# Mixtures of experts: the standardized rows stored by SyncE on the hardware queue, ahead of the experts' weights

## What is computed

```
x = x + mamba(layernorm(x))
x = x + mixture0(layernorm(x))      # 32 experts, top 4
x = x + rotary_attention(layernorm(x))
x = x + mixture0(layernorm(x))
x = x + sink_attention(layernorm(x))
x = x + mixture1(layernorm(x))      # 48 experts kept, top 8, at most 96 rows each
x = x + latent_attention(layernorm(x))
x = x + mixture1(layernorm(x))
```

## Time and profile before

| | |
|---|---|
| median of 3 executions | 4134.72 us (4134.48 to 4136.27) |
| the profiled execution | 4140.78 us |
| its span, first to last instruction | 4138.2 us |
| PE busy | 3287.4 us, 79% of the span |
| DVE busy | 2811.4 us, 68% |
| ACT busy | 2274.7 us, 55% |
| POOL busy | 1809.1 us, 44% |
| mean granted PE clock | 0.871 |

### The profile page before, as it was taken

The page is one execution under the profiler, slowest core; times in us unless marked ns, Lnnn a source line. Parts: engine busy times, 40 slices in busy tenths (PEclk is TensorE's granted clock), DMA queues, the critical chain, the costliest instruction groups (busy, mean ns, idle before and its releaser), DMA issues. The chain is left out here.

```text
span 4138.2 us, 68603 instructions
## 1 busy us (share of the span) xinstructions
PE 3287.4 (79%) x19706; PEld 2595.8 (63%) x19707; DVE 2811.4 (68%) x6227; ACT 2274.7 (55%) x5958; POOL 1809.1 (44%) x3103
## 2 busy tenths in 40 slices
PE   7799958916888499089999999999737399999374
PEld 3355546715777377068778878788635288888253
DVE  5699956636777566468768778588553388888542
ACT  3599913405777244078768678688302266666021
POOL 0299923567663144636446356255237200000265
PEclk9799978958999599589999999999856699999566
DMA  2011132430000335300000000000234300000524
GB/s 84 20 48 49 49 144 89 136 101 13 1 1 1 144 114 131 113 29 19 17 11 20 14 14 19 11 17 20 112 86 67 102 1 1 1 1 1 180 51 105
DMA packets 133309, 221.35 MB, mean 53 GB/s; under 512 B 28912, under 2 KB 106608, under 8 KB 131264
## 3 DMA queue, kind: packets, MB, share of 16 engines
q1 hardware_dynamic: 99216, 147.84, 10.7%
q0 software_dynamic: 33792, 69.83, 7.4%
HBM read 162.60 MB, written 54.80 MB: 53 GB/s over the span
## 5 line engine op out<-in xcount | busy, mean ns | idle before, releaser
L1271 POOL DMA_INDIRECT ex_xr<-scratch_rows,mo_token x288 | 287.5, 998 | 324.8 <-issue 289.1
L596 POOL TENSOR_TENSOR sc_h<-sc_h,sc_c 128x512 f32<-128x512 f32 x256 | 327.2, 1292 | 198.1 <-DVE sc_h L633 190.2
L3044 DVE TENSOR_TENSOR sa_pT<-bank,sa_pT 128x512 fp32r<-128x512 f32 x512 | 329.9, 686 | 34.4 <-ACT sa_pT L2912 30.5
L2904 ACT ACTIVATE sa_p<-bank,sa_nm 128x512 f32<-128x512 f32 x512 | 346.9, 689 | 2.5 <-DVE sa_nm L3035 2.5
L633 DVE TENSOR_TENSOR_SCAN sc_h<-sc_da,bank 128x512 f32<-128x512 f32 x256 | 311.1, 1220 | 38.4 <-ACT sc_da L576 23.5
L2733 PE MATMUL bank<-sa_kT,sa_qT 128*128 128x512 f32 x1024 | 332.7, 436 | 1.5 <-DVE residual L3011 1.5
L3031 DVE TENSOR_REDUCE sa_mx<-bank 128x2 f32<-128x1024 f32 x256 | 312.4, 1220 | 25.6 <-PE bank L2735 21.7
L1337 PE MATMUL bank<-mo_w_gu,ex_xT 128*128 (+2 forms) x1152 | 315.0, 402 | 1.1 <-issue 0.6
L2757 PE MATMUL bank<-sa_pT,sa_v 128*128 128x256 f32 x2048 | 301.4, 290 | 17.1 <-DVE sa_pT L3044 16.4
L2757 PEld LDWEIGHTS bank<-sa_pT,sa_v 128*128 128x128 f32 x2048 | 260.2, 190 | 40.0 <-DVE sa_pT L3044 31.4
L2912 ACT ACTIVATE sa_pT<-bank 128x512 fp32r<-128x512 f32 x512 | 274.3, 585 | 7.7 <-PE bank L2745 0.5
(11 more groups left out here) (402 smaller groups left out, 9458.5 us busy)
## 6 DMA issues: line engine op xcount, KB each, us to landing
scratch_ys<-ex_yo SPq DMA_DIRECT2D x192, 128.0 KB
mo_w_gu<-in_w_gu SPq DMA_DIRECT2D x2, 9216.0 KB, 26.2
sc_c<-scratch_c SPq DMA_DIRECT2D x64, 256.0 KB, 3.1
sa_share<-scratch_shares SPq DMA_DIRECT2D x256, 64.0 KB, 2.6
mo_w_dn<-in_w_dn SPq DMA_DIRECT2D x2, 4608.0 KB, 47.5
mo_w_dn<-in_w_dn SPq DMA_DIRECT2D x2, 4096.0 KB, 34.7
scratch_rows<-ln_stage POOLq DMA_DIRECT2D x64, 128.0 KB, 21.9
ex_xr<-scratch_rows,mo_token POOLq DMA_INDIRECT x288
```

Of the source, the lines that this page charges most:

```text
L596: pool.tensor_tensor(h, h, C[u], ALU.mult).then_inc(used.sem, 1)
L1271: pool.indirect_dma_start(xr[u][:, :], None, rows, bass.IndirectOffsetOnAxis(ap=token[:, i:i + 1], axis=0), bounds_check=rows.shape[0] - 1 ...
L2904: act.activation(pr[h][:, :], SC[2 * s_ + h][:, :], ACT.Exp, bias=nm[:, col:col + 1], scale=SCALE, accum_out=rs[:, col:col + 1]).then_inc( ...
L3044: dve.tensor_tensor(spot(1), PT[h][:, :].rearrange("p (k n) -> p k n", k=TPB), spot(0).bitcast(F32), ALU.subtract).then_inc(*inc("kept_d"))
```

## The change

POOL no longer stores the standardized rows. SP does it, between `loads` and `late_loads`: for each tile it waits until DVE has made it and issues the store. Then come the experts' weights (and the copy of the residual). Last, SP waits within the block until all 16 stores have landed.

```diff
@@ -179,16 +179,16 @@
                         loads(sp)
                     if not c.fills:
                         zero_scratch(c, sp)
+                    if rows is not None:
+                        for i in range(TILES):
+                            sp.wait_ge(normed.sem, normed.at(i + 1))
+                            sp.dma_start(rows[0][i * P:(i + 1) * P, 0:D_MODEL], normal(i)) \
+                              .then_inc(rows[1][i % 4].sem, 16)
                     if late_loads is not None:
                         late_loads(sp)
-
-            if rows is not None:
-                @block.gpsimd
-                def _(pool):
-                    for i in range(TILES):
-                        pool.wait_ge(normed.sem, normed.at(i + 1))
-                        pool.dma_start(rows[0][i * P:(i + 1) * P, 0:D_MODEL], normal(i)) \
-                            .then_inc(rows[1][i % 4].sem, 16)
+                    if rows is not None:
+                        for u in range(4):
+                            sp.wait_ge(rows[1][u].sem, rows[1][u].at(16 * (TILES // 4)))
```

## The result

The changed kernel takes 4073.7 us (median of 4, 4072.2 to 4076.4) against 4135.5 us (median of 4, 4134.5 to 4141.4): a ratio of 0.985, 95% interval 0.983 to 0.987, or 62 us less. The forecast was 4075 us, with a range of 4066 to 4088.

What follows compares the result with a forecast made beforehand. Taken to bound the kernel: four waits, 62.3 us in all, at router openings, until POOL's row stores land. Less 4 x 0.6 us, the gain is 59.9, all other terms nil: 4134.7 - 59.9 = 4074.8 us, range 4066 to 4088.

Steps and rivals of the forecast that it cites:

- The cause of the holes: Router block's opening: all engines idle, 62.3 us in four waits, because POOL ends the layer-norm block only when its stores land.
- The first rival: Layer-norm block's end: rows land as late as before, since all queues share 16 DMA engines; no change, 4134.7 us; chance 0.03.
- The gain term: Four router openings: waits of 62.3 us shrink to 0.6 us each, a gain of 59.9 us.
- SP's issues: Layer-norm block: 16 added stores on SP per mixture at 0.4 us each, ending at 575.5 and 2991.9; no cost.
- The other stand-in: Layer-norm block: each row's store lands 3.5 us after its issue, as the tags do, the last at 579.0.
- The margins: Layer-norm block's end: rows land before DVE's last work by 12 us in the first mixture, 10 us in the third.
- The weights: Issued 16 to 17 us later, behind the stores; slack 36 us before PE, 16 us before POOL's first gather; no cost.
- The tags: Router block, second kind: behind the copy on SP's queue, landing by 3052.2 at the latest, slack 11 us; no cost.
- Load beside the router: Router's first 12 us (first kind) to 42 us (second) run under the weights' load; taken as 0, up to 7.8 us.

Runs made afterwards that it cites:

- `only_second_kind`: Against the kernel before: SP stores the rows in the two mixtures of the second kind alone, POOL still stores in the first kind; 4091.5 us, ratio 0.989.
- `pool_rows_made_first`: Against the kernel before: POOL still stores the rows, SP issues the weights once DVE has made the last tile; 4179.9 us, ratio 1.010.
- the last experiment: Against the changed kernel: SP issues weights and copy in the router block, only after DVE has counted the masks; 4103.6 us, ratio 0.992.
- `sp_weights_first`: Against the changed kernel: SP issues the weights and copy first and the row stores behind them, still waiting for the rows; 4144.6 us, ratio 1.0024.
- `copy_on_pool`: Against the changed kernel: in the second kind POOL issues the residual's copy after DVE's last tile, nobody in the block waiting for it; 4078.1 us, ratio 0.986.

## Why the prediction was right

**The cause of the holes.** The reading that POOL does not come to the end of a block before its own stores are done rested on two coincidences, given as 0.9 us; the landings unrounded make them 1.0. The trace before has them in all four mixtures: DVE goes on 0.98 to 0.99 us after POOL's last row is in. The two runs in which POOL stores beside the load (`only_second_kind` in its first kind, `pool_rows_made_first` in all four) have 0.97 to 0.98, for holes between 7.7 and 35.2 us. It is now shown by a transfer that was put there for the test and waited for by nobody in the block, with holes of 38.6 and 38.9 us up to 0.4 us past its landing. SP's transfers do not hold the block: in the changed kernel `mo_w_dn` is under way until 608.0 and the copy until 3020.3, and the blocks end at 586.9 and 2981.4 with 0.3 us of waiting. What makes POOL wait, the engine by itself or something that stands at the end of its list, the profile does not say.

**What the change does.** The diff does two things that might gain, and no term of the prediction tells them apart: it moves the stores to another queue, and it puts them ahead of the weights. The runs tell them apart. Order alone: all of the gain (4074.5 beside 4075.4). Queue alone, with SP's wait for the rows: a loss of 9 us (4144.6 beside 4135.2); without that wait a gain of some 7 us by the estimate above, not run. The rule of the Trainium skill's page "DMA: Bandwidth & Descriptors" ("Issuing engines are not separate DMA queues"), by which the choice of the engine saves only time of issuing, agrees with this: on a quiet queue the stores land in 2.2 us from POOL and 1.9 from SP. The first rival took the rule for a reason of no change, and was wrong in that the order had changed too.

**The gain term.** 62.3 us, less the cost of a plain opening. I took that as 0.6 us, from openings after other blocks; it is 0.3 here, so the term is 61.1 and not 59.9. The work up to DVE's last index was indeed not moved: from the first load it takes 33.1 us before and after in the first mixture, and 36.7 and 36.6 in the third. The 1.2 us between the two terms are the difference between forecast and result, as far as the scatter lets one say.

**SP's issues.** 0.40 us each were taken; they are 0.49 with the wait (7.85 us for 16). The other stand-in was off the other way: a store lands in 1.9 us, where the tags had 3.5. The two errors nearly cancel, which was luck: the last row is in 9.3 us after the first issue (564.3, 571.7 + 1.9), where 9.9 and 10.4 were worked out. The margins, given as 12 and 10 us, are 13.0 and 11.4, and twice the stores cost nothing.

**The weights.** In the third mixture the copy lands at 3020.3 against a gather at 3039.4: 19 us of slack where 16 were given. It takes 51.0 us in place of 55.9. That the rows are now out of its way is the likely reason: in the third mixture it took 50.6 to 51.9 wherever SP issued it and no row of POOL was under way beside it, and 53.1 in `pool_rows_made_first`. That the loss past the slack is one for one, and only in the second kind, is borne out by the last experiment: of the 15.7 us by which the load is later, 13.0 are lost, and the rest was what remained of the slack. The order's price is nil while the slack is there.

The rule "Overlap DMA with compute" of the Trainium skill's page "DMA: Bandwidth & Descriptors" ("Rules for kernel authors") says to issue a transfer early and to wait late; here the early issue of the weights cost 61 us, because something smaller and more urgent was under way beside it, and 17 to 18 us later, counted from DVE's first standardized tile, was early enough.

**The tags.** That they would be behind the copy was foreseen, not that SP would be stuck in their issue. It costs nothing, as SP has nothing else to do there.

**Load beside the router.** Taken as nothing, with 7.8 us for the range. The prediction has the load over the first 12 us of the router in the first kind; that is counted from the router's old start, and its own 610.2 against the new one, 591.8, makes 18. The trace has 21 (608.0 less 586.9), and 39 in the second kind, where 42 were given. The routers last 52.0, 51.9, 58.0 and 57.7 us against 51.9, 51.9, 58.1 and 57.7.

## What to carry to other kernels

If all engines wait at the end of a block and no semaphore explains it, look for a transfer of POOL and compare its landing with the time at which they go on. Put small urgent stores ahead of a large load with slack, whichever queue they are on; and do not start the load while some of them are still out: with POOL's stores that was the worst of all the orders. When an edit moves a thing to another queue it often moves it in the order too, so one of the two must be tried alone before either is praised.

## What was not expected of the hardware

- POOL's transfers beside a load that SP has already queued fare very unevenly. A 2048 KB copy issued 4 us before the weights landed in 10.6 us; issued 10 us after them it took 40.5, to 2.8 us past the weights' own landing. In every block with such a hole POOL's last transfer landed 0.2 to 5.3 us after `mo_w_dn`. POOL's last 128 KB stores took 30.6 us behind a load that had started 4 us earlier, and 2.2 us without one. What decides is open; that it is not the transfer's own bytes is plain, since the smaller ones took longer than the 10.6 us of the larger.
- SP can be held in the issue of a transfer for long. The tags' issue takes 0.37 us on a quiet queue, and 16.9, 20.8, 28.7, 30.8 and 45.7 us behind the weights and the copy in various states. The weights themselves, far more bytes, take 0.45 us to issue each. In all nine runs that have this hold, in both mixtures of the second kind, the tags' issue ends 0.03 to 0.34 us before `mo_w_dn` lands: at 3015.07 against 3015.10 in the changed kernel. In `sp_weights_first` it is the first row's issue that takes 36.2 us in the third mixture, to within 0.1 us of that landing. After such a hold the tags land some 7 us after the end of their issue (23.6 - 16.9); on a quiet queue they land 3.5 us after its start. With the copy given to POOL (`copy_on_pool`) SP is not held, though both weights are still under way until 3029.7:

```profile
3006.16 0.38 SPq L967 DMA_DIRECT2D scratch_rows<-mo_tags  x1
```

So the two weights ahead do not hold the tags by themselves here; with the copy there too they do. The rows show that it is not the bytes of the waiting transfer. Whether the number of pieces decides (the tags have 2048 of 64 bytes) was not tried.
